# The weight column of the gated rows written by GpSimd, two tiles ahead, instead of by ScalarE; the sorted keys stored in two halves

## The reference

```python
xn = _layernorm(x)
# gnn: neigh = xn[dst]; w = sigmoid(relu(neigh @ W1 + b1) @ W2 + b2)
#      num = segment_sum(neigh * w, src); den = segment_sum(w, src); num / den where den > 0
# mix: kv = einsum(ln(k), ln(v)) / N per head; out = q @ kv + xn
x = x + _L0_gnn_ref(xn, [src, dst], ...) + _L0_mix_ref(xn, ...)
x = x + _L0_ffn_ref(_layernorm(x), ...)      # top 2 of 6 experts for each row
```

## Time and profile before

| | before |
|---|---|
| median of 3 runs | 1635.37 us (1631.89 to 1641.35) |
| the profiled execution, its time | 1637.26 us |
| its span in the trace | 1635.4 us |
| busy: PE, DVE, ACT, POOL | 86%, 81%, 50%, 38% |
| stretch 2 (turns of levels 16 to 18) | 325 to 439 us |
| tiles 0 to 48 written by ACT | 342.33 to 433.2 us |

### The profile page before, as it was taken

How to read it: one execution, slowest core, us unless ns; L and a number is a source line. 1 busy time by engine, 2 the same in 40 slices (tenths; PEclk the granted TensorE clock), 3 DMA queues, 4 the chain that set the end, 5 groups by cost and what they waited for, 6 DMA issues and landing times.

```text
span 1635.4 us, 39521 instructions
## 1 busy us (share of the span) xinstructions
PE 1405.0 (86%) x12059; PEld 1319.1 (81%) x12059; DVE 1324.4 (81%) x3945; ACT 821.0 (50%) x2011; POOL 614.8 (38%) x617
## 2 busy tenths in 40 slices
PE   0147888756499999999999999999999499999997
PEld 0136787656389999999999999999999499999996
DVE  9999899999678888888888888888888666666665
ACT  3123455358645555555555555555555255555553
POOL 2663657574312222222222222222222243335565
PEclk9767899767799999999999999999999799999999
DMA  9000000039851111111111111110111254444553
GB/s 203 6 1 1 1 1 1 1 90 216 191 156 40 38 49 39 48 39 47 40 39 51 36 48 39 45 45 35 48 39 47 105 174 137 130 121 81 86 92 54
DMA packets 78244, 108.73 MB, mean 66 GB/s; under 512 B 14622, under 2 KB 60683, under 8 KB 77927
## 3 DMA queue, kind: packets, MB, share of 16 engines
q1 hardware_dynamic: 50342, 56.99, 12.9%
q0 software_dynamic: 27408, 50.18, 12.4%
q10 hardware_dynamic: 432, 0.79, 0.1%
HBM read 45.34 MB, written 57.47 MB: 63 GB/s over the span
## 4 chain that ended last, share of the span: by engine, by line
PE 72%; DVE 17%; issue 3%; POOL 2%; DMA 2%; ACT 2%; DVEq 1%; POOLq 0%; SPq 0%; ACTq 0%
PE turned L1407 19%; PE front L1407 18%; DVE sort_mem L1707 12%; PE turned L1389 9%; PE turned L1546 6%; PE front L1546 6%; PE front L1566 5%; DVE sort_mem L1715 2%; PE turned L1539 1%; PE front L1436 1%; PE front L1429 1%; PE turned L1346 1%; PE front L1292 1%; PE front L1296 1%; DVE acc_mem L1670 1%
## 5 line engine op out<-in xcount | busy, mean ns | idle before, releaser
L1804 DVE TENSOR_TENSOR sort_mem<-lane_bf,sort_mem 128x512 bf16<-128x512 bf16 x1372 | 518.2, 419 | 123.5 <-PE turned L1389 112.2
L1143 ACT ACTIVATE a_ring<-turned 128x384 fp32r<-128x384 f32 (+1 forms) x686 | 373.6, 545 | 377.7 <-PE turned L1389 374.9
L1407 PE MATMUL turned<-y_all,a_ring 128*128 128x258 f32 x2450 | 387.4, 296 | 0.7 <-ACT a_ring L1143 0.7
L1407 PE MATMUL front<-y_all,a_ring 128*128 128x258 f32 x2352 | 376.4, 296 | 0.0
L1407 PEld LDWEIGHTS turned<-y_all,a_ring 128*128 128x128 f32 x2450 | 318.2, 191 | 1.1 <-ACT a_ring L1143 1.1
L1707 DVE TENSOR_TENSOR sort_mem<-sort_mem 128x320 f32<-128x320 f32 (+2 forms) x568 | 312.1, 611 | 3.0
L1407 PEld LDWEIGHTS front<-y_all,a_ring 128*128 128x128 f32 x2352 | 306.0, 190 | 0.0
L1389 PE MATMUL turned<-sort_mem 128*128 128x128 bf16 (+1 forms) x2695 | 259.9, 217 | 2.4 <-DVE sort_mem L1804 2.1
L966 POOL DMA_INDIRECT out_rows<-base x108 | 145.6, 1348 | 158.7 <-DVE base L2116 92.9
L1389 PEld LDWEIGHTS turned<-sort_mem 128*128 128x128 bf16 x2695 | 139.7, 98 | 39.3 <-DVE sort_mem L1804 8.1
L1346 PE MATMUL turned<-ident,sort_mem 128*128 128x128 f32 x286 | 55.3, 353 | 100.6 <-DVE sort_mem L1707 99.6
(11 more groups left out here) (262 smaller groups left out, 1982.4 us busy)
## 6 DMA issues: line engine op xcount, KB each, us to landing
base<-token_lists SPq DMA_DIRECT2D x54, 258.0 KB, 2.8
base<-token_lists SPq DMA_DIRECT2D x54, 130.0 KB, 2.5
y_all<-tab_mem POOLq DMA_DIRECT2D x49, 129.0 KB, 3.8
gated_rows<-tab_mem SPq DMA_DIRECT2D x49, 128.5 KB, 3.2
late_mem<-mixed_rows SPq DMA_DIRECT2D x49, 128.0 KB, 2.0
mixed_rows<-base SPq DMA_DIRECT2D x12, 512.0 KB, 3.8
feat_mem<-in_L_ffn_expert_w SPq DMA_DIRECT2D x18, 256.0 KB, 6.1
base<-in_x SPq DMA_DIRECT2D x1, 3136.0 KB
```

Source lines behind the costliest of these rows:

```text
L1143: nc.scalar.activation(a_ring[:, k % 2, :, :].rearrange("p s n -> p (s n)")[:, 0:width], ps_a[k % 2][:, 0:width], ACT.Copy).then_inc(S["a_ ...
L1407: last = nc.tensor.matmul(ps_agg[odd], a_ring[:, k % 2, n, :], y_part(t, part), start=(t == 0 and part == 0), stop=(t == BLOCKS - 1 and pa ...
L1804: nc.vector.tensor_tensor(hot[:, k % 2, 0:pairs, :, :], lane_bf[:, :, :].unsqueeze(1).broadcast_to([P, pairs, P, 2]), edges.unsqueeze(2).b ...
```

## The change

The weight column is no longer written by ACT behind the features. POOL writes it (`write_weight`), for tiles 0, 1 and 2 ahead of the first accumulating DMA, and then for tile t+2 ahead of the accumulating DMA of tile t. A new semaphore, `w_ready`, is waited for by ACT ahead of the high part and by SP ahead of the gated store. The store of the sorted keys is split: the first half (8 of 13 chunks) is stored as soon as it is sorted, the second when it is.

```diff
             for t in range(FULL):
                 if t == KEPT_AFTER + 1:
-                    for half in range(2):
+                    for half, tiles in enumerate((slice(0, HALF // P), slice(HALF // P, TILES))):
                         sp.wait_ge(sorted_half[half], instructions_before(LEVELS, -1, half))
-                    sp.dma_start(kept_chunks, ordered_chunks).then_inc(S["kept_stored"], 16)
+                        sp.dma_start(kept_chunks[:, tiles, :], ordered_chunks[:, tiles, :]).then_inc(S["kept_stored"], 16)
                 sp.wait_ge(S["y_ready"], t + 1)
+                sp.wait_ge(S["w_ready"], t + 1)
...
+            def write_weight(t):
+                s = t % Y_SLOTS
+                if t >= Y_SLOTS:
+                    pool.wait_ge(y_stored[s], 16 * (t // Y_SLOTS))
+                    pool.wait_ge(low_added[s], 16 * (t // Y_SLOTS))
+                nc.gpsimd.tensor_copy(y_out[:, s, DIM:ROW], gate[:, t:t + 1]).then_inc(S["w_ready"], 1)
+
+            write_weight(0)
+            write_weight(1)
             for t in range(BLOCKS):
+                if t + 2 < BLOCKS:
+                    write_weight(t + 2)
                 pool.wait_ge(S["parts_ready"], t + 1)
                 nc.gpsimd.dma_start(y_part(t, 1), y_out[:, t % Y_SLOTS, :], accum_op=ALU.add).then_inc(low_added[t % Y_SLOTS], 16)
...
-            pool.wait_ge(S["kept_stored"], 32)
+            pool.wait_ge(S["kept_stored"], 48)
...
-                nc.scalar.activation(y_out[:, s, 0:DIM], base[:, t, :], ACT.Identity, bias=y_bias[:, t:t + 1], scale=y_scale[:, t:t + 1])
-                nc.scalar.activation(y_out[:, s, DIM:ROW], gate[:, t:t + 1], ACT.Copy).then_inc(S["y_ready"], 1)
+                nc.scalar.activation(y_out[:, s, 0:DIM], base[:, t, :], ACT.Identity, bias=y_bias[:, t:t + 1],
+                                     scale=y_scale[:, t:t + 1]).then_inc(S["y_ready"], 1)
                 act.wait_ge(S["y_ready"], t + 1)
+                act.wait_ge(S["w_ready"], t + 1)
```

More of the change, by code:

```diff
@@ L505, in gps_layer @@
             mix_ps mix_done mixed_stored mixed_loaded
-            dst_lane_ready slot_step parts_ready kept_stored below_ps
+            dst_lane_ready slot_step w_ready parts_ready kept_stored below_ps
             count_ready key_at_ready key_held window_in unkeyed_ready found_ready lanes_ready valid_ready lanes_f_ready edges_turned
@@ L633, in _ @@
             sp.wait_ge(S["y_ready"], BLOCKS)
+            sp.wait_ge(S["w_ready"], BLOCKS)
             sp.dma_start(y_table[FULL * P:BLOCKS * P, :], y_out[:, 0, 0:ROW]).then_inc(y_stored[0], 16)
@@ L1175, in act_alone @@
                     act_pieces(n, j)
-            act.wait_ge(S["kept_stored"], 32)
+            act.wait_ge(S["kept_stored"], 48)
             act.wait_ge(S["lanes_ready"], 2)
```

## The result

The changed kernel takes 1664.51 us (median of 6 runs, 1659.91 to 1670.81) against 1636.79 us for the kernel before (6 runs beside it): a ratio of 1.0168, with a 95% interval of 1.0146 to 1.0191, so 27.7 us or 1.7% slower. The forecast was slower by 0.7%, 1647 us, with a range up to 1659: the sign held, the size did not. The execution profiled took 1670.81 us, 6.3 us above its median, so its rows show a somewhat larger loss than the medians do.

What follows compares the result with a forecast made beforehand. The end of DVE's sort, set by ACT's tiles ahead of its last turn, was taken to bound the kernel; 10.6 + 0.7 - 0.1 = +11.2 us gave 1648.5 for the profiled execution, 1647 us as median, range 1637 to 1659.

Steps and rivals of the forecast that it cites:

- T(t) = T(t-2) + P: POOL's accumulating DMA of tile t waits for tile t-2's landing; P, landing 3.4 plus 0.7, is 4.1 us per two tiles.
- rival A: The forecast itself: POOL's chain of two DMAs binds, P between 3.75 and 4.6, +4 to +21 us; chance 0.70.
- d: Time from a landing to POOL's next DMA issue: wait, copy, issue and DVE's blocking, 0.7 us, bounds 0.35 and 1.2.
- 10.6 us: Delay of ACT's copy for the sort's last turn, (18,6), by POOL's chain: 434.0 against 423.35.
- The signs: What the profile would show: longer ACT and DVE waits, POOL's copy waiting 40 to 60 us, sort ending near 450.
- T(0): Start of tile 0's accumulating DMA on POOL, behind the attention matrix and first weight: 351.4 against 350.35 before.
- a copy that arrives at any moment in an exchange ... waits half of one, 0.28 us: POOL's weight copy beside DVE's exchanges of 0.48 to 0.68 us: mean wait 0.28 us, at most one whole exchange.
- rival B: Landings of accumulating DMAs stay at 4.1 us, so P is 4.8: +24.7 us, 1660 us; chance 0.09.
- Rival D: ACT also waits for late weights at the high part; adds only the copy, 0.3 us, once; counted inside rival A.
- DVE's stretching, +0.7: In the last 15 us six POOL copies hold DVE's sort 0.1 to 0.18 us each: +0.7 us.
- the keys, -0.1: Storing sorted keys by halves wins at most 0.2 us, since POOL's gather also waits for DVE's key positions: -0.1.
- Rival C: POOL's chain does not bind (P under 3.5), ACT sets the last turn: 1633.6 us; chance 0.21 including small unmeasurable losses.

Runs made afterwards that it cites:

- drained: The changed kernel, with DVE waiting for its own last half-0 exchange once per pass in the sort's last three levels; 1646.87 us, ratio 1.0063.
- chain_only: The kernel before, ACT writing the weight, POOL only waiting for tile t-2's landing ahead of tile t's DMA, without a copy; 1648.0 us, ratio 1.0070.
- memset_after: The changed kernel, with a memset of 1.0 on POOL in place of the weight copy, so nothing is read; 1647.04 us, ratio 1.0054.
- copy_only: The kernel before, with POOL copying one column into an unused tile ahead of each DMA, and no wait for a landing; 1638.18 us, ratio 1.0003.
- port measurement: No layer computed: five stages of 72 DVE instructions, a 128x1 GpSimd copy or memset at every fourth; one copy held for 7.4 us.

## Why the forecast had the sign and not the size

**T(t) = T(t-2) + P, rival A: the mechanism was right, and P nearly so.** From the starts and landings of tiles 0 to 38, 19 links each, a link takes 4.20 us in drained, whose copies run beside exchanges and are not held (forecast 4.1): 3.53 of landing and 0.67 of d, near my 3.4 and 0.7. But d is made of other parts than I thought. It is 0.52 us in chain_only, without any copy, 0.57 in memset_after and 0.67 in drained. So waiting and issuing cost 0.5 us, where I had 0.25, and DVE cost 0.1, where I had 0.28. (The four DMAs issued back to back lie 0.13 us apart, not 0.10.)

**That 10.6 us lies near the 11.7 of chain_only is in part luck.** The 10.6 holds a copy in every link and 1.05 us for a later first tile, and chain_only has neither: for it I expected P = 3.6 and 2 to 8 us, and P was 4.15, 3.6 of it landing, where the expectation had 3.3. A chain adds up its landings, so their mean counts, not their median. And what the sum for (18,6) lacked is the mixed batch behind tile 41, 1.00 us at 429.29 in chain_only; for (17,6) and (18,17) it had counted one.

**The signs.** ACT waited 50.6 us at the features and at the high part together (forecast over 25), DVE 13.8 us at (17,6) (about 5) and 19.3 at (18,6) (about 11.5). POOL's wait for landings at L858 was 32.4 us, below the 40 to 60 of the forecast; in memset_after, where no copy is held while DMAs land, it was 39.1.

**The first tile.** T(0) was 353.2, not 351.4; 1.6 us of that is that the attention matrix ended at 351.6 instead of 350.02.

**The step that failed: "a copy that arrives at any moment in an exchange ... waits half of one, 0.28 us", with "a whole exchange" as its upper bound.** For most copies it holds: the median of all is 0.24 us, and but for one of 0.99 us they last at most 0.68. For three of 49 it does not: they waited until DVE's run broke, 24.0 us together. A mean over copies is also the wrong number for this: one held copy stops DMA issue and, through `w_ready`, ACT at once. The 24.0 us became 17.6 us of stretch against drained (97.8 against 80.2), whose own waits cost up to 2.3, and 18.8 against memset_after. Less than 24.0, I take it, since ACT and POOL find slots free when the hold ends; no run separates this. This took the result past rival B's 1660, by another road: the landings did not stay at 4.1.

**Rival D, "this adds only the copy, 0.3 us": wrong for the same reason.** It is the wait through which a held copy reaches ACT, 8.98, 4.50 and 9.01 us of it.

**What I could have read.** The trace before had it: the groups of POOL's products, which also read SBUF (min/median/max ns):

```profile
L801 POOL TENSOR_TENSOR acc_mem<-acc_mem x25: 917/1052/32745, 67.9 to 327.0; 128x512 f32<-128x512 f32 x24, 128x256 f32<-128x256 f32 x1
L797 POOL TENSOR_TENSOR acc_mem<-acc_mem,gath_mem x25: 2112/3236/9707, 64.6 to 324.8; 128x16 f32<-128x16 f32 x24, 128x8 f32<-128x8 f32 x1
```

A maximum of 32.7 us at a median of 1.05 is an instruction that was held. In order of time it stands beside DVE's exchanges:

```profile
67.92 32.74 POOL L801 TENSOR_TENSOR acc_mem<-acc_mem 128x512 f32<-128x512 f32 x1
```

From 65.7 us on, DVE's exchanges, with all inputs in SBUF, follow each other without a gap up to 99.76, where one starts 0.035 us behind the end of the one before. The product ended at 100.67, 0.9 us behind that break. So the sort of the kernel before had already held a GpSimd instruction for some 32 us. I bounded the wait by a row of L831 at 1.35 us and read no maximum.

The Trainium skill ("SBUF — State Buffer", section "Who interferes with whom") says that the ports which DVE and GpSimd share are an exclusive lock, and that whoever issues first holds them for the whole instruction. That much is what 15 of 16 copies in the port measurement show. It would end every wait with DVE's present instruction, at most 0.68 us; the held copies of 3.4 to 16.4 us contradict it, and the measurement decides.

**DVE's stretching, +0.7, and the keys, -0.1.** The keys gave 0.03 us, within the 0.2 allowed. The stretching is too small to read beside the held copies; DVE's exchanges within the stretch took 51.0 us for 100 in both kernels.

**Rival C** (the chain does not bind) fell with chain_only, which is slower by 0.5% to 0.9% through the chain alone. **Rival B** (landings stay at 4.1) fell with the landings of the changed kernel, 3.3 us median.

## What to carry to other kernels

A tiny GpSimd instruction that reads SBUF is not cheap beside DVE instructions with two SBUF inputs that follow each other without a gap: price it by the maximum of such rows, not the median, as a hold of up to DVE's whole run, and ask who waits for it (in copy_only nobody did, and it cost nothing that the medians show). If it must be there, write without reading (a memset), give DVE a gap once in a while, or let nothing on the critical path wait for it. And writing k tiles ahead into n slots leaves only n-k transfers in flight: count that before moving a write to the queue that issues them, and price the chain by the mean of its landings.

## What the runs showed of the hardware that was not expected

- A 128x1 GpSimd copy was held off over 12 (7.39 us) and, in runs of 32 DVE instructions, over some 27 of them (16.4 us), and always until the run ended or a gap came; a gap for DVE's wait for its own instruction is enough (longest copy 0.54 us in that stage of the port measurement, 0.88 us in drained).
- It is a matter of when the copy asks, and regular: of copies that ask 6 ns or so apart and just miss an instruction's end, every fifth was held, six in all.
- A memset of the same column took 0.099 us beside DVE with two SBUF inputs, and a copy 0.185 us beside DVE with one PSUM input. Beside DVE with one SBUF input a copy took 0.35 us, and there even a memset of 8 columns took 0.32 us instead of 0.10:

```profile
135.38 0.32 POOL L80 MEMSET pad<- 128x8 f32 x1 [5.93 <-DVE o L58]
```
